# Radial products spread over both steps of a pair, a new order on VectorE and ScalarE, and one weighted tile a step

## The reference

```
h       = relu(layernorm(x))
message = (h @ w_src + b_src)[src] + (h @ w_dst)[dst]
rad     = silu(silu(edge_attr @ w1 + b1) @ w2 + b2) @ w3 + b3        # the radial layers
message = (message * edge_weight * rad) @ w_sep + b_sep              # 8 heads x (16 alpha + 16 value)
score   = sum_k smooth_leaky_relu(alpha) * alpha_dot
att     = softmax of score over the edges of one destination
out     = x + (segment_sum(value * att, dst)) @ w_proj + b_proj
```

## Time and profile before

| | |
|---|---|
| median of 3 runs | 5225.42 us (5225.09 to 5227.14) |
| the profiled execution | 5225.56 us, its span 5223.8 us |
| PE busy | 4870.1 us, 93% of the span |
| DVE busy | 3883.1 us, 74% |
| POOL busy | 3649.5 us, 70% |
| ACT busy | 2757.9 us, 53% |
| granted TensorE clock, mean | 0.976 |

### The profile page before, as it was taken

One profiled execution on the slowest core, in us unless ns is written; L12 is line 12 of the kernel. 1 busy time (PEld: TensorE's weight loads), 2 busy tenths in 40 slices (PEclk: granted clock), 3 DMA queues, 4 the chain that ended last, 5 costly groups with the idle time before them and its releaser, 6 DMA issues. The chain is left out here.

```text
span 5223.8 us, 92056 instructions
## 1 busy us (share of the span) xinstructions
PE 4870.1 (93%) x28995; PEld 3532.0 (68%) x28995; DVE 3883.1 (74%) x6981; ACT 2757.9 (53%) x3939; POOL 3649.5 (70%) x3491
## 2 busy tenths in 40 slices
PE   3589999999999999999999999999999999999975
PEld 2456777777776777777777777777767777777754
DVE  6547777777777777777777777777777777777777
ACT  2455555555555555555555555555555555555511
POOL 2377777777777777777777777777777777777716
PEclk9799999999999999999999999999999999999975
DMA  6666666666666666666666666666666666666625
GB/s 186 188 194 197 203 194 206 199 200 203 197 205 196 204 201 198 204 196 204 199 200 203 199 202 197 202 201 200 203 200 199 195 205 202 202 198 203 198 67 156
DMA packets 889678, 1019.19 MB, mean 195 GB/s; under 512 B 161780, under 2 KB 778008, under 8 KB 888863
## 3 DMA queue, kind: packets, MB, share of 16 engines
q1 hardware_dynamic: 758843, 774.32, 46.2%
q0 software_dynamic: 108784, 223.44, 16.6%
q10 hardware_dynamic: 21556, 15.50, 1.1%
HBM read 863.59 MB, written 152.34 MB: 194 GB/s over the span
## 5 line engine op out<-in xcount | busy, mean ns | idle before, releaser
L1056 POOL DMA_INDIRECT gath<-msg_src,idx x3328 | 3506.5, 1054 | 1271.3 <-issue 1103.6
L1241 ACT ACTIVATE sil<-a_ps,ba 128x512 f32<-128x512 f32 x832 | 572.5, 688 | 1315.7 <-PE a_ps L1355 1308.3
L1360 PEld LDWEIGHTS v_ps<-wv,msgT 128*128 128x128 f32 x6656 | 863.6, 191 | 416.3 <-issue 260.2
L1176 DVE TENSOR_TENSOR msgT<-xT_ps,rads 128x512 f32<-128x512 f32 x832 | 572.6, 688 | 654.0 <-PE xT_ps L1340 650.9
L1355 PE MATMUL a_ps<-msgT,wa 128*128 128x512 f32 x1664 | 931.1, 641 | 116.1 <-DVE msgT L1176 115.8
L1295 PE MATMUL rad_ps<-wval,hot 128*128 128x136 f32 x6656 | 930.1, 284 | 37.9 <-DVE wval L1147 34.6
L1360 PE MATMUL v_ps<-wv,msgT 128*128 128x128 f32 x6656 | 880.9, 275 | 0.0
L1295 PEld LDWEIGHTS rad_ps<-wval,hot 128*128 128x128 f32 x6656 | 847.9, 194 | 43.3 <-DVE wval L1147 38.4
L1190 DVE SCALAR_TENSOR_TENSOR sil<-a_ps,sil 128x512 f32<-128x512 f32 x832 | 568.0, 683 | 190.7 <-ACT sil L1241 182.4
L1284 PE MATMUL xT_ps<-hotT,win 128*128 128x256 f32 x3328 | 643.1, 315 | 0.0
L1123 DVE SCALAR_TENSOR_TENSOR rads<-rad_ps,b,rows_bc 128x1024 f32<-128x1024 f32 x416 | 532.4, 1280 | 127.7 <-PE rad_ps L1273 127.2
(11 more groups left out here) (234 smaller groups left out, 4496.9 us busy)
## 6 DMA issues: line engine op xcount, KB each, us to landing
rows_bc<-edge_rows SPq DMA_DIRECT2D x416, 768.0 KB
win<-msg_dst SPq DMA_DIRECT2D x1664, 128.0 KB
sums<-run SPq DMA_DIRECT2D x416, 272.0 KB
attr<-in_edge_attr_t SPq DMA_DIRECT2D x1664, 32.0 KB
gath<-msg_src,idx POOLq DMA_INDIRECT x3328
msg_dst<-dst_parts SPq DMA_DIRECT2D x98, 128.0 KB, 2.1
pen_g<-pen_rows SPq DMA_DIRECT2D x208, 32.1 KB
mask_g<-mask_rows SPq DMA_DIRECT2D x208, 32.0 KB
```

The costliest lines, as they stand in the source:

```text
L1056: pool.indirect_dma_start(gath[:, u, s], None, msg_src, bass.IndirectOffsetOnAxis(ap=idx[:, j // 8, at:at + 1], axis=0)).then_inc(s_gath[u ...
L1176: dve.tensor_tensor(msgT[:, j % 2], xT_ps[:, :], rads[:, j % 4], ALU.mult).then_inc(s_msg, 1)
L1241: act.activation(sil[:, j % 8], a_ps[:, :], ACT.Silu, bias=ba[:, :]).then_inc(s_sil, 1)
L1360: last = pe.matmul(v_ps[:, s * P:(s + 1) * P], lhsT=msgT[:, q, s * P:(s + 1) * P], rhs=wv[:, :], start=True, stop=True)
```

## The change

The three radial products leave the end of the odd step. `z1(k + 2)` is cut in two halves of one product each (two matmul records), one in the even and one in the odd step, between the transposes and `aggregate`; `z2(k + 1)` goes to the even step after the value product; `radial(k + 1)` goes in the odd step between the alpha and the value product. On VectorE `scale_rad` moves from the end of the odd step to right behind `accumulate`, ahead of `weigh` and of the alpha sum; `weigh` makes one tile a step; in even steps `mark` comes ahead of `accumulate`; the softmax part comes last in odd steps; and the second scan and the small products behind it move from steps 3 and 4 to 4 and 5. On ScalarE `second` and the last part of `prepare_hotT` move to the odd step, `first` to the end of the odd step, the exponentials behind `first`, and the first part of `prepare_hotT` (`measure`) stays in the even step.

```
 VectorE, step:
                     if there(t):
                         dve.wait_ge(s_xT, t + 1)
+                        if j % 2 == 0:
+                            dve.wait_ge(s_rads, t // 2 + 1)
                         dve.tensor_tensor(msgT[:, j % 2], xT_ps[:, :], rads[:, j % 4], ALU.mult).then_inc(s_msg, 1)
                     if group(g - 1) and j == 14:
                         soft(g - 1, j)
-                    if there(t - LAG):
-                        accumulate(*later(g, j, -LAG))
                     if j % 2 == 0:
                         if there(t + 2 - LAG):
                             mark(*later(g, j, 2 - LAG))
-                    elif there(t + 1 - LAG):
+                        if there(t - LAG):
+                            accumulate(*later(g, j, -LAG))
+                        if group(g - 1) and j != 14:
+                            soft(g - 1, j)
+                    else:
+                        if there(t - LAG):
+                            accumulate(*later(g, j, -LAG))
+                        if there(t + 1):
+                            scale_rad(*later(g, j, 1))
+                    if j != 12 and there(t + 1 - LAG):
                         weigh(*later(g, j, 1 - LAG))
-                    if group(g - 1) and j != 14:
-                        soft(g - 1, j)
+                    if j == 11 and there(t + 2 - LAG):
+                        weigh(*later(g, j, 2 - LAG))
                     if there(t):
                         dve.wait_ge(s_sil, t + 1)
                         dve.scalar_tensor_tensor(sil[:, j % 8], a_ps[:, :], 0.25, sil[:, j % 8], ALU.mult, ALU.add).then_inc(s_al, 1)
-                        if j % 2 and there(t + 1):
-                            scale_rad(*later(g, j, 1))
+                    if j % 2 and group(g - 1):
+                        soft(g - 1, j)
 VectorE, weigh: one multiplication of one tile, then_inc(s_wv, 1), in place of two
 VectorE, soft: the part of j == 3 is that of j == 4 now, that of j == 4 is that of j == 5
 TensorE, step:
                     if there(t):
-                        if j % 2 == 0:
-                            pe.wait_ge(s_rads, t // 2 + 1)
                         pe.wait_ge(s_gath[j % U], 64 * (4 * g + j // U) + 64)
                         for s in range(SUB):
                             last = pe.matmul(xT_ps[...], ...)
                         last.then_inc(s_xT, 1)
+                        if there(t // 2 * 2 + 4):
+                            z1(t // 2 + 2, q)
+                        if q == 0:
+                            pe.wait_ge(s_rads, t // 2 + 1)
...
                         pe.matmul(a_ps[:, :], lhsT=wa[:, :], rhs=msgT[:, q], start=True, stop=True).then_inc(s_a, 1)
+                        if q and there(t + 1):
+                            need(pe, s_run, 2 * (t - LAG) + 2)
+                            radial((t + 1) // 2)
                         need(pe, s_vout, t)
...
                         last.then_inc(s_v, 1)
-                        if q:
-                            k = t // 2
-                            need(pe, s_run, 2 * (t - LAG) + 2)
-                            if k + 1 < NPAIR:
-                                radial(k + 1)
-                            if k + 2 < NPAIR:
-                                z2(k + 2)
-                            if k + 3 < NPAIR:
-                                z1(k + 3)
+                        if q == 0 and there(t + 2):
+                            z2(t // 2 + 1)
                         if there(t + 1):
                             dst_part(*later(g, j, 1))
 TensorE, aggregate: waits for s_wv in each step, no longer in even ones alone
 ScalarE, step:
                         copy_values(*later(g, j, -1))
-                    if there(t) and j % 2 == 0:
-                        k = t // 2
-                        if k + 1 < NPAIR:
-                            second(k + 1)
-                        if k + 2 < NPAIR:
-                            first(k + 2)
+                    if j % 2 and there(t + 1):
+                        second((t + 1) // 2)
+                        prepare_hotT(*later(g, j, 1))
...
                         act.activation(sil[:, j % 8], a_ps[:, :], ACT.Silu, bias=ba[:, :]).then_inc(s_sil, 1)
+                    if j % 2 and there(t + 3):
+                        first((t + 3) // 2)
...
-                    if there(t) and j % 2 == 0 and there(t + 2):
-                        prepare_hotT(*later(g, j, 2))
+                    if j % 2 == 0 and there(t + 2):
+                        measure(*later(g, j, 2))
```

More of the change, by code:

```diff
@@ L1072, in soft @@
                         dve.tensor_tensor_scan(fwd[:, :], pen[:, 0:TE], shifted[:, :], -BIG, ALU.add, ALU.max).then_inc(s_soft, 1)
-                    elif j == 3:
+                    elif j == 4:
                         dve.tensor_tensor_scan(bwd[:, :][:, ::-1], pen[:, 1:TE + 1][:, ::-1], shifted[:, :][:, ::-1], -BIG, ALU.add, ALU.max).then_inc(s_soft, 1)
@@ L1076, in soft @@
                         dve.tensor_scalar(ends[:, 0:G], sel[:, :], fwd[:, TE - 1:TE], None, ALU.mult).then_inc(s_soft, 1)
-                    elif j == 4:
+                    elif j == 5:
                         dve.wait_ge(s_soft, k + 4)
@@ L1141, in weigh @@
                         need(dve, s_agg, a - 2)
-                        if j == 0:
-                            dve.wait_ge(s_wT, g + 1)
+                    if j == 0:
+                        dve.wait_ge(s_wT, g + 1)
                     slot = G * (g % 2) + j
[L1145 to L1149, removed]
+                    at = 32 * (j % 4) + H * (j // 4)
+                    dve.tensor_tensor(wval[:, u], vals[:, slot], wT[:, :, at:at + H].unsqueeze(3).broadcast_to((P, SUB, H, HV)), ALU.mult).then_inc(s_wv, 1)
                 def accumulate(g, j):
@@ L1209, in second, with measure, prepare_hotT @@
                     act.activation(h2[:, :], z_ps[:, 1, :], ACT.Silu, bias=b2[:, :]).then_inc(s_h2, 1)
-                def prepare_hotT(g, j):
-                    t = G * g + j
-                    k = t // 2
+                def measure(g, j):
+                    k = (G * g + j) // 2
                     act.wait_ge(s_rows[k % 2], 80 * (k // 2) + 80)
                     act.activation(apart[:, :, :], rows_bc[:, k % 2, :, 0:REL_W].bitcast(bf16), ACT.Square, bias=row_below[:, :]).then_inc(s_apart, 1)
-                    act.wait_ge(s_apart, k + 2)
-                    need(act, s_D, t - 2)
+                def prepare_hotT(g, j):
+                    act.wait_ge(s_apart, (G * g + j) // 2 + 2)
                     act.activation(hotT[:, j % 4:j % 4 + 2].rearrange("p n (i e) -> p (n i) e", i=2), apart[:, :, :], ACT.Relu, bias=1.0, scale=-1.0).then_inc(s_hotT, 1)
@@ L1237, in step @@
                         act.wait_ge(s_wp, n + 1)
+                        need(act, s_wv, G * n)
                         act.activation(wT[:, :, :].rearrange("p s n -> p (s n)"), v_ps[:, :], ACT.Copy).then_inc(s_wT, 1)
@@ L1246, in step @@
                         act.activation(drop[:, :], drop[:, :], ACT.Exp).then_inc(s_exp, 1)
-                    if there(t) and j % 2 == 0 and there(t + 2):
-                        prepare_hotT(*later(g, j, 2))
+                    if j % 2 == 0 and there(t + 2):
+                        measure(*later(g, j, 2))
                 act.activation(row_below[:, :], row_number[:, :], ACT.Copy, scale=-1.0).then_inc(s_apart, 1)
                 act.wait_ge(s_apart, 1)
+                measure(0, 0)
+                prepare_hotT(0, 0)
                 first(0)
@@ L1253, in _ @@
                 first(1)
-                prepare_hotT(0, 0)
                 stream(act, step)
@@ L1258, in _, with z1 @@
             def _(pe):
-                def z1(k):
+                def z1(k, r):
                     u = k % (UA // 2)
[L1261 to L1265, removed]
+                    if r == 0:
+                        pe.wait_ge(s_attr[u], 64 * (k // (UA // 2)) + 64)
+                        need(pe, s_h1, k)
+                    product = pe.matmul(z_ps[:, 0, CE * r:CE * (r + 1)], lhsT=w1[:, r], rhs=attr[:, 2 * u:2 * u + 2].rearrange("p i e -> p (i e)"),
+                                        start=True, stop=True)
+                    if r:
+                        product.then_inc(s_z1, 1)
                 def z2(k):
@@ L1270, in radial @@
                 def radial(k):
+                    pe.wait_ge(s_h2, k + 1)
                     for n in range(2):
@@ L1289, in aggregate @@
                     a = G * g + j
-                    if j % 2 == 0:
-                        pe.wait_ge(s_wv, a // 2 + 1)
+                    pe.wait_ge(s_wv, a + 1)
                     for i in range(2):
@@ L1361, in step @@
                         last.then_inc(s_v, 1)
-                        if q:
-                            k = t // 2
-                            need(pe, s_run, 2 * (t - LAG) + 2)
-                            if k + 1 < NPAIR:
```

(18 more changed lines are left out.)

## The result

The changed kernel takes 5243.03 us (5239.98 to 5245.52, 7 runs) against 5225.42 us: ratio 1.0034, 95% interval 1.0022 to 1.0045. Its profiled execution has a span of 5240.9 us, 17.1 more than before. A later run of both gave 1.0031 (1.0019 to 1.0044). So it is slower, by half of what was forecast.

A forecast was written before the change was run, and what follows sets the result against it. TensorE was taken to set the pace, losing time waiting for the message, with GpSimd close behind. From 5225.6 us: +27 in the loop, -6 in the first 30 tiles, +13 in the tail, giving 5260 us, range 5235 to 5300 (63%).

The forecast's parts named there:

- The chain from radial to the message: VectorE between radial and the next message in odd steps: alpha product possible 4.33 us after radial, TensorE there at 4.35.
- The new waits: TensorE late by 0.63 us in step 2, 0.6 in step 6, 1.17 in step 10, 0.55 in step 11; 2.95 a group.
- TensorE's own work: Same matmuls in new order: even step 5.0 us, odd step 5.4, pair still 10.4; 89.2 us a group without message waits.
- No gain, no loss: Odd steps, aggregate to radial: 1.98 us against 2.02 before; bounds minus 0.1 to plus 0.2 us an odd step.
- the +27 us: Loop from first aggregate to last message, 50 groups: 2.4 us of waits go, 2.95 come, 92.15 us a group.
- The first tiles: First 30 tiles: GpSimd holds the gain at 10.0 us a pair against some 10.4; -6 us.
- The tail: Last 30 steps: one tile weighed a step, each aggregate waited for alone, about 0.9 us a pair; +13 us, bounds 0 and 17.
- The first, that `radial` comes early: Rival: alpha weights load ahead or radial starts 0.1 us sooner a pair; 91.3 to 91.6 us a group, 5215 to 5235 us; 15%.
- The second, no waits: Rival: VectorE keeps up and message waits vanish; 89.2 us a group, about 5113 us; 8%.
- the third: Rival: radial's two waits and tile size changes cost 0.2 us an odd step, 1.6 a group; 5340 us; 10%.
- GpSimd did not become the bound: Rival that it would: gathers, slowed by VectorE, pass 1.44 us each and set the pace; about 5360 us; 4%.

## Why the prediction was right, and where its size was off

**The chain from radial to the message** was right, step by step. `scale_rad` starts 1.18 us after `radial` (4052.31, 4053.49) and the message of step 10 4.81 us after it, 3.6 + 1.19 forecast. The new waits, from the starts of all groups: 0.65 us in step 2, 0.64 in step 6, 1.18 in step 10, 0.61 in step 11 (about half of it at the aggregate, which the forecast had all at the message), in sum 3.1 us for 2.95 forecast; those of steps 3 and 11 of before are gone. That the softmax part is what makes the wait is shown for step 10 (5.00 us) and, in few groups, for step 6 (5.24) by moving it; for steps 2 and 11 it rests on the arithmetic, which hits to 0.02 and 0.06 us.

**TensorE's own work** is the term that was mis-sized: "No gain, no loss" from aggregate to `radial`. I had the 2.02 us of before against 1.98; measured are 1.93 (4050.38 to 4052.31). An odd step takes 5.33 us and not 5.4. Without waits a group is 91.76 less 3.1, about 88.7 us, where I had kept 89.2. So a group went from 91.6 to 91.76 and not to 92.15: 9.6 us in place of 27. The two waits ahead of `radial` cost 0.05 us behind the end of the sums (4051.90 + 0.36), and I had put 0.1. This term, paid in eight odd steps a group, is what the +27 us were too high by; the new waits came out 0.1 us a group above the forecast and not below it.

**The first tiles** gave 6.6 us, 6 forecast. **The tail** cost 14.7 us, 13 forecast. The waits are the forecast ones, 2.27 us and, where `mark` covers part, 1.14:

```profile
5076.26 0.35 DVE L1163 SCALAR_TENSOR_TENSOR run<-run,keep,rad_ps 128x136 f32<-128x136 f32 x1 [1.14 <-PE rad_ps L1304]
...
5077.69 2.18 PE L1304 MATMUL rad_ps<-wval,hot 128*128 128x136 f32 x8 [1.47 <-DVE wval L1146]
...
5079.91 0.36 DVE L1163 SCALAR_TENSOR_TENSOR run<-run,keep,rad_ps 128x136 f32<-128x136 f32 x1 [2.27 <-PE rad_ps L1304]
```

But 2.27 us is what a wait takes at half the clock, where the aggregate takes 2.18 us and not the 1.09 of the loop. The row from which I took it stands at half the clock too, and my sum has no term for the clock, which was 0.57 over the tail in place of 0.68. How much of the 14.7 us is the clock's isn't shown; that 13 came so near is in part luck.

**The rivals.** The first, that `radial` comes early, was half true: 0.1 us earlier, and 0.5 us a group with it, which took away over half of the loss. The weights of the alpha product do load ahead,

```profile
4051.20 0.31 PEld L1366 LDWEIGHTS a_ps<-msgT,wa 128*128 128x128 f32 x2
```

0.11 us before it, but that isn't what set `radial`'s start: the sums end 0.05 us before it. The second, no waits, is refuted by 98 of them, the third by the 1.93 us. GpSimd did not become the bound: in the changed kernel it still waits for TensorE, and a gather costs (2240.3 + 639.3) / 2093 = 1.38 us.

```profile
L1056 POOL DMA_INDIRECT gath<-msg_src,idx x2093 | 2240.3, 1070 | 760.0 <-issue 639.3 <-PE xT_ps L1347 120.7
```

**What the change gives and takes.** It takes the late starts of steps 3, 11 and 15 away (0.72, 1.52 and 0.14 us, 2.4 a group) and 0.5 us of TensorE's own time. It puts `radial` so close to the next message that VectorE's softmax parts of three odd steps stand in the chain, and that of step 10 between two messages, and gives 3.1 us back.

## What to carry to other kernels

When a producer is moved closer to its consumer, add up everything that the engine between them does in that gap, side work too, and put the side work ahead of the wait: here VectorE sat idle 1.23 us for `radial` and then did 1.19 us of softmax behind it. That this removes the wait is shown in undisturbed steps; a gain of that size in the whole time is not. Half-sized hand-overs that cost little where other work lies between them double the waits in the tail, where nothing else is left to do; keep the larger unit there.

## What was not expected of the hardware

The tail's length goes with the granted clock, and that with how busy TensorE is kept. With one tile a step TensorE was busy 63 of 110 us and granted 0.57, with two and `mark` inside the wait 46 of 77 us and 0.82, before 57 of 95 us and 0.68. The same work, the aggregates of 30 tiles, so keeps TensorE busy for 46 to 63 us. Which of the two comes first, idle time or clock, no run separates. And the same kernel took 5226 us on some chips and about 6300 on others, where VectorE, ScalarE and GpSimd also wait up to several us for something whose releaser the profile does not know; why is open. Which order of steps is best may differ between them: by the estimate above the change that costs 0.3% on the first kind gains 1.6% on the other, and two scans of the kernel before, moved, cost 0.4 to 0.5% there, though the waits that they had caused were gone in undisturbed groups.
